# A graph-network kernel whose indirect DMAs are held, at the third of every four, until the four before them have landed

## The reference

```python
h = jnp.maximum(_layernorm(x, axis=-1), 0.0)
x = x + layer(h, ...)
```

## Time and profile before

| | |
|---|---|
| median of 3 runs | 13379.83 us (13370.13 to 13388.96) |
| the profiled execution | 13428.51 us, its span 13426.7 us |
| mean granted clock of TensorE | 0.649 |
| busy share of the span | PE 50%, PEld 41%, DVE 41%, ACT 19%, POOL 48% |
| indirect DMAs | 4992 gathers (six stretches of 832) and 1564 scatters (two of 782) |
| DMA queues' share of 16 engines | POOL's 19.1%, SP's 1.8% |

### The profile page before, as it was taken

One profiled execution on the slowest core, in us unless ns is written; L12 is line 12 of the kernel. 1 busy time (PEld: TensorE's weight loads), 2 busy tenths in 40 slices (PEclk: granted clock), 3 DMA queues, 4 the chain that ended last, 5 costly groups with the idle time before them and its releaser, 6 DMA issues. The chain is left out here.

```text
span 13426.7 us, 153123 instructions
## 1 busy us (share of the span) xinstructions
PE 6728.9 (50%) x36515; PEld 5521.2 (41%) x36516; DVE 5467.3 (41%) x19680; ACT 2491.4 (19%) x7971; POOL 6482.5 (48%) x6770
## 2 busy tenths in 40 slices
PE   5333575666665000987355548888533333333333
PEld 2111243566665000865244437888422222222222
DVE  7444368233332000321455555777533333233333
ACT  0000100222221000011155545777300000000000
POOL 3555100444333777000166634666466656665665
PEclk8666555677777555555566779999755555555555
DMA  0000000111111000000111128999311121121112
GB/s 27 2 2 2 24 27 2 34 31 29 27 27 20 1 1 1 6 2 0 33 44 44 44 51 292 325 322 324 128 46 46 46 44 46 46 45 45 46 46 48
DMA packets 390372, 797.87 MB, mean 59 GB/s; under 512 B 163641, under 2 KB 199938, under 8 KB 389762
## 3 DMA queue, kind: packets, MB, share of 16 engines
q0 software_dynamic: 302976, 715.02, 19.1%
q1 hardware_dynamic: 86850, 79.63, 1.8%
q10 hardware_dynamic: 320, 0.80, 0.0%
HBM read 729.05 MB, written 65.95 MB: 59 GB/s over the span
## 5 line engine op out<-in xcount | busy, mean ns | idle before, releaser
L155 POOL DMA_INDIRECT edge_rows<-tab,all_slots x3328 | 3258.1, 979 | 1709.5 <-issue 906.2
L1666 PE MATMUL edge_psum<-edge_rows,edge_onehot 128*128 128x128 f32 x4992 | 1191.2, 414 | 2448.8 <-DVE edge_onehot L1645 1953.6
L1666 PEld LDWEIGHTS edge_psum<-edge_rows,edge_onehot 128*128 128x128 f32 x4992 | 1026.8, 305 | 2613.1 <-DVE acc_acc L1655 1535.9
L786 POOL DMA_INDIRECT all_x<-tab_src,all_slots x832 | 787.1, 946 | 2007.8 <-SPq L777 916.4
L1655 DVE TENSOR_TENSOR acc_acc<-acc_acc,edge_psum 128x128 f32 x2496 | 716.3, 287 | 2489.5 <-remote 2039.2
L155 POOL DMA_INDIRECT edge_rows<-tab,edge_slots x832 | 815.1, 980 | 1714.7 <-DMA edge_slots<-slots_s 1250.9
L1535 PE MATMUL edge_p_m<-edge_rows,edge_onehot 128*128 128x128 f32 x9984 | 1180.4, 278 | 195.5 <-DVE edge_rows L1502 96.7
L1535 PEld LDWEIGHTS edge_p_m<-edge_rows,edge_onehot 128*128 128x128 f32 x9984 | 1140.6, 193 | 235.4 <-issue 189.8
L456 POOL DMA_INDIRECT slots_d<-all_slots,pro_row_d x782 | 751.0, 960 | 682.1 <-DVE pro_row_d L558 453.4
L1467 ACT ACTIVATE edge_rows<-edge_rows,edge_coef 128x128 f32<-128x128 f32 x3328 | 995.1, 387 | 374.4 <-DMA edge_rows<-tab,all_slots 350.5
L954 POOL DMA_INDIRECT slots_s<-acc_pays,acc_row_s x782 | 801.5, 1025 | 339.1 <-issue 268.7
(11 more groups left out here) (338 smaller groups left out, 11971.1 us busy)
## 6 DMA issues: line engine op xcount, KB each, us to landing
edge_rows<-tab,all_slots POOLq DMA_INDIRECT x3328
tab<-tab_o SPq DMA_DIRECT2D x50, 512.0 KB, 2.6
all_x<-tab_src,all_slots POOLq DMA_INDIRECT x832
edge_rows<-tab,edge_slots POOLq DMA_INDIRECT x832
tab_src<-all_x SPq DMA_DIRECT2D x50, 260.0 KB, 2.0
slots_d<-all_slots,pro_row_d POOLq DMA_INDIRECT x782
slots_s<-acc_pays,acc_row_s POOLq DMA_INDIRECT x782
tab<-acc_own SPq DMA_DIRECT2D x15, 640.0 KB, 3.6
```

What stands on the lines that cost most here:

```text
L155: pool.indirect_dma_start(out=rows[:, slot, j, :], out_offset=None, in_=table[:, :], in_offset=bass.IndirectOffsetOnAxis(ap=index, axis=0) ...
L786: pool.indirect_dma_start(out=rows[:, (g % R0) * G + j, :], out_offset=None, in_=D["tab_src"][:, :], in_offset=bass.IndirectOffsetOnAxis(a ...
L1666: m = pe.matmul(psum[:, slot % 2, j * P:(j + 1) * P], onehot[:, slot % 2, j, :], rows[:, slot, j, :], start=True, stop=True)
```

## The change

In `gather_groups` and in edges0, POOL waits before the third of each group's four gathers, from the second group on, until all gathers of the group before have landed. The wait is on the semaphore of that group's ring place, whose count is 16 for each gather and turn of the ring. Scatters are grouped in fours likewise (`scatter_columns`): the two semaphores of a sort now alternate by groups of four columns instead of single ones, so that one semaphore tells that a group has landed, and the third scatter of each group waits for the group before. SP's waits for all scatters get the number of columns that each semaphore now counts (`columns_of`: 392 and 390 instead of 391 each).

```diff
--- before.py
+++ after.py
@@ -146,14 +146,31 @@
 def gather_groups(pool, ring, freed, gathered, parts):
 
 
+
+    each = 16 * G * len(parts)
     for g in range(GROUPS):
         slot = g % ring
         wait(pool, freed, g - ring + 1)
         for j in range(G):
+            if j == G // 2 and g:
+                pool.wait_ge(gathered[(g - 1) % ring], each * ((g - 1) // ring + 1))
             for rows, table, slots, field in parts:
                 index = slots[:, G * g + j, field:field + 1].bitcast(I32)
                 pool.indirect_dma_start(out=rows[:, slot, j, :], out_offset=None, in_=table[:, :],
                                         in_offset=bass.IndirectOffsetOnAxis(ap=index, axis=0)).then_inc(gathered[slot], 16)
+
+
+def scatter_columns(pool, semaphores, c):
+
+
+    g, j = divmod(c, G)
+    if j == G // 2 and g:
+        pool.wait_ge(semaphores[(g - 1) % 2], 16 * G * ((g - 1) // 2 + 1))
+    return semaphores[g % 2]
+
+
+def columns_of(z):
+    return sum(1 for c in range(EC) if c // G % 2 == z)
 
 
 def flat(ap):
@@ -424,7 +441,7 @@
                 sp.wait_ge(stored_a[z], 16 * (NW // 2))
 
             for z in range(2):
-                sp.wait_ge(K["scattered"][z], 16 * (EC // 2))
+                sp.wait_ge(K["scattered"][z], 16 * columns_of(z))
             sp.dma_start(K["slots"][:, :, :], D["slots_d"][0:SLOTS, :].rearrange("(p t) f -> p t f", t=TILES)).then_inc(q["slots_in"], 16)
             sp.wait_ge(q["slots_in"], 16)
 
@@ -453,8 +470,9 @@
             for c in range(EC):
                 if c % (COLS * BATCH) == 0:
                     pool.wait_ge(q["rows_d"], c // (COLS * BATCH) + 1)
+                done = scatter_columns(pool, K["scattered"][0:2], c)
                 pool.indirect_dma_start(out=D["slots_d"][:, :], out_offset=bass.IndirectOffsetOnAxis(ap=row_d[:, c:c + 1], axis=0),
-                                        in_=payd[:, c, :], in_offset=None).then_inc(K["scattered"][c % 2], 16)
+                                        in_=payd[:, c, :], in_offset=None).then_inc(done, 16)
 
         @block.scalar
         def _(act):
@@ -783,6 +801,8 @@
             for g in range(GROUPS):
                 wait(pool, q["freed"], g - R0 + 1)
                 for j in range(G):
+                    if j == G // 2 and g:
+                        pool.wait_ge(gathered[(g - 1) % R0], 16 * G * ((g - 1) // R0 + 1))
                     pool.indirect_dma_start(out=rows[:, (g % R0) * G + j, :], out_offset=None, in_=D["tab_src"][:, :],
                                             in_offset=bass.IndirectOffsetOnAxis(ap=slots[:, G * g + j, F_SRCT:F_SRCT + 1].bitcast(I32), axis=0)).then_inc(gathered[g % R0], 16)
 
@@ -946,13 +966,14 @@
             sp.dma_start(D["tab1"].rearrange("(w p) c -> p w c", p=P), rows).then_inc(q["stored"], 16)
             sp.wait_ge(q["stored"], 16)
             for z in range(2):
-                sp.wait_ge(K["scattered"][2 + z], 16 * (EC // 2))
+                sp.wait_ge(K["scattered"][2 + z], 16 * columns_of(z))
 
         @block.gpsimd
         def _(pool):
             for c in range(EC):
+                done = scatter_columns(pool, K["scattered"][2:4], c)
                 pool.indirect_dma_start(out=D["slots_s"][:, :], out_offset=bass.IndirectOffsetOnAxis(ap=K["row_s"][:, c:c + 1], axis=0),
-                                        in_=K["pays"][:, c, :], in_offset=None).then_inc(K["scattered"][2 + c % 2], 16)
+                                        in_=K["pays"][:, c, :], in_offset=None).then_inc(done, 16)
 
         @block.tensor
         def _(pe):
```

## The result

The changed kernel takes 13616.67 us (median of 4 runs, 13609.64 to 13621.53), against 13377.09 us for the kernel before (4 runs): 1.0178 of before, interval 1.016 to 1.0195. The forecast was 11110 us. The change is **slower by 240 us**, and of the forecast gain of 2270 us nothing came.

A forecast was written before the change was run, and what follows sets the result against it. Unbroken indirect DMAs from POOL were taken to make PE's results reach other engines late. Terms summed to −2270 from the profiled 13428.5, giving 11158, or 11110 us on the runs' scale; range 10950 to 12900.

The forecast's parts named there:

- The step that failed: All gather and scatter stages: the hold limits POOL's instructions ahead to four, so its queue never fills.
- a full queue of POOL starves PE: Sort, middle, edges3: while POOL's queue stands full, something PE needs is served once per POOL instruction; full cure 0.57.
- the rival: All stretches: POOL's being busy, not its queue, makes PE late; POOL streams as before, 13380 us; chance 0.14.
- −616: Prologue, sort by destination: 49 batches of four picks without stall take 633 us instead of 1249.
- −1009: Middle: relation loop takes 493 us, the middle ends at 5623, and its scatters hide beneath.
- −190: Edges1: 1278 us against 1039 POOL-bound, with 50 us of standing still kept; −100 to −215.
- −435: Edges3: each of three stages falls from 1206.6 to 1061 us, 3 × −145.
- +10: Edges2: the hold binds by up to 1.3 us a group, mostly absorbed by DMA busy 0.92; 0 to +270.
- The landing of scatters: Scatter stages: last DMA activity 0.5 to 1.0 us behind the last instruction's end, leaving 1.5 us to spare.
- slower: Edges2: its hold binds, 1.3 us × 208 = +270, with POOL's being busy as cause; 13650 us; chance 0.09.
- Partly cured: Sort, middle, edges1, edges3: four ahead still too many, the lag only halves; 11500 to 12900 us; chance 0.20.
- no change: All stretches: the hold is fulfilled before it is due and PE stays late; 13380 us; chance 0.14.

The follow-up runs named there:

- e2: The changed kernel with the hold taken out of edges2 alone: 13372.62 us, 0.9989 of the kernel before.
- e5: The kernel before; in the middle alone each scatter waits until the one two before has landed: 13387.97 us, 0.9995.
- e3: The kernel before; in the middle alone POOL waits ahead of every fourth scatter until all so far have landed: 12456.57 us, 0.9294.
- e4: The kernel before; in the middle alone each scatter waits until the one before has landed: 13020.01 us, 0.9708.
- e10: The kernel before with a drain per 4 scatters in the sort, a POOL fill per 4 in the middle, various holds in edges1 to edges3: 12127.18 us, 0.9054.

## Why the prediction was wrong

**The step that failed** is "with the hold, at most the two left of a group and two of the next are ahead", with the theory it served, that a full queue of POOL starves PE. The hold did bound what stands ahead, as said, and it was free in seven stretches, as said (e2: 0.9989). But PE did not care: e5 bounds it tighter and changes nothing (0.9995). What frees PE is a real gap between the indirect DMAs (e3, e4, e10), and the hold makes none in those seven. I had the observation that contradicts it in the text, as the case for the rival: in the sort DVE gets its result after the last scatter of a batch, with nothing queued. From the pauses in the trace I had read that pauses cure, and then priced a wait that makes none. The terms of prologue, middle, edges1 and edges3 (−616, −1009, −190, −435) all came to nothing: none of these stretches moved by more than 9 us.

**The observation itself was right, and its sizes too.** Where a real gap was put in, the sort's picks took 638 us (633 forecast) and the relation loop 490 (493). On chips where PE is never late the kernel before takes 10835 to 10847 us: 2540 less, of which some 200 are edges2's. Edges3 takes 1060 us there from the first gather to the last addition (1061 forecast). One reading of the trace was incomplete: edges2 does have late signals, of some 2 us, ahead of POOL's first gathers and of DVE.

**Edges2 was mis-sized**: +10 taken, 0 to +270 given, +267 measured. The bound was 1.3 us × 208; the third gathers wait 2.3 us, 1.5 us of pause ahead of the first disappears, and POOL's gathers are 0.5 us longer per group, which I had at nothing. That the bound of 270 was met so closely is luck. I trusted the busy share of 0.92 to absorb the hold. It doesn't, since only two gathers are under way when it ends, and the DMA engines run dry until the next two are issued: 0.02 busy from 8710.0 to 8710.5, 0.81 over the stage.

**The landing of scatters was read too short.** The last DMA activity lies 0.5 to 1.0 us behind the last scatter's end, but e4's trace has the landing 2.1 us after the start, 1.1 behind the end. The holds were fulfilled even so. The Trainium skill's fixed 2.0 us per DMA ("DMA: Bandwidth & Descriptors", anatomy of one SWDGE DMA) agrees with these 2.1 us. It was not what decided; 4.8 us of landing under load in edges2 were.

**The rival that came true** is the one called slower, with 0.09: POOL's streaming stays as it is, and edges2's hold binds; 13650 forecast, 13617 measured. It was right in what it foresaw and not in its cause, POOL's being busy: e10 excludes that. The mark given for it, edges2's pitch near 7.8 us, is what the profile shows, and so are relation groups 30 us apart. "Partly cured" (11500 to 12900) and "no change" are excluded by the measured interval, 1.016 to 1.0195. The chances were wrong: two rivals rested on one cause, for which the trace spoke more clearly than for mine, and got 0.23. One sum of the partial case is wrong as well: with −430 in the middle and all the other terms in full it gives 11690, not 11600.

## What to carry to other kernels

Before a wait is meant to relieve something, work out whether it is ever unfulfilled when due; one that is always fulfilled changes nothing, and one that binds on a stage near its DMA limit lets the DMA engines run dry, at a price of landing plus issue per group. If an engine's signals come late while another streams indirect DMAs, put a real gap between them where slack hides it: here a drain per four scatters (a gap of 1.9 us) gained 939 us, and a fill with a gap of 1.67 us cured the same loop. Leave the streams that set a stage's length alone, and time it on more than one chip. Drains and fills in the sort and the middle gained 7% (e3) on one kind, and 9% in e10 in spite of its costly holds in edges3; on the other kind they cost 0.3 to 0.8%.

## What the runs showed of the hardware that was not expected

- The same program takes 13377 to 13407 us (medians) on one kind of chip (or in one condition of it) and 10835 to 10847 on another. The runs don't tell what sets the kind.
- On the first kind PE's results reach other engines some 20 us late while POOL issues indirect DMAs 0.30 us apart. It is the DMAs (a fill of 1.5 us in between cures it), not the depth of the queue (e5), and not POOL's being busy. A gap of 0.55 us per four, or one of 0.49 that is longer at one fill in four, gives little or nothing; 1.67 us per four gives all, 2 us per eight most in the relation loop and all in edges3. What in the chip stands behind it stays open.
- Without such gaps the lag is regular: in the middle 33.6 us from group to group in the traces of before and of e5, 24 to 25 scatters of 1.37 us, and a group is 24 instructions of PE and PEld. That is near one per scatter; no run varied that number.
- A gather of edges2 that starts 0.1 us behind DVE's L1511 takes 1.94 us instead of 0.93.
- 4 KB rows move at 324 GB/s (busy 0.92) on the first kind and 384 (1.00) on the second, yet both come to 270 and 1618 to 1620 us when each group waits for the one before.
